# Attention: the three bf16 parts of the negated row maxima laid out as part, head, tile, and turned into rows by one TensorE transpose of 48 columns instead of four of 12

## What is computed

```python
attn = einsum('bhqd,bhkd->bhqk', q, k) * scale          # layer 1
attn = where(causal, attn, -inf)
a = clip(attn, -100.0, 100.0)
m = max(a, axis=-1, keepdims=True)
e = exp(a - m)
p = e / (sum(e, axis=-1, keepdims=True) + 1e-06)
p = p + 1e-08
attn = p / sum(p, axis=-1, keepdims=True)

scores = einsum('bqhd,bkhd->bhqk', q, k) * scale        # layers 2 and 4
probs = softmax(scores, axis=-1)
```

## Time and profile before

| | us |
|---|---|
| median of 3 runs | 2610.97 |
| lowest and highest | 2608.83 and 2614.83 |
| the profiled execution | 2617.94 |
| its span, first to last instruction | 2616.2 |

### The profile page before, as it was taken

How to read it: one execution, slowest core, us unless ns; L and a number is a source line. 1 busy time by engine, 2 the same in 40 slices (tenths; PEclk the granted TensorE clock), 3 DMA queues, 4 the chain that set the end, 5 groups by cost and what they waited for, 6 DMA issues and landing times. The chain is left out here.

```text
span 2616.2 us, 46472 instructions
## 1 busy us (share of the span) xinstructions
PE 2440.0 (93%) x15044; PEld 1418.3 (54%) x15044; DVE 1836.5 (70%) x3685; ACT 1439.2 (55%) x2991; POOL 1350.9 (52%) x1358
## 2 busy tenths in 40 slices
PE   6999999999999999989899699987999999989998
PEld 3555555554444444349799366653344444358897
DVE  4989998999778888844343558867778888844333
ACT  3666666666777777653233223214777777653332
POOL 5356665563234545445555569843334445435555
PEclk8999999999999999999999789988999999999999
DMA  5333333333434444234555200015434444245554
GB/s 159 100 100 108 105 102 105 111 99 101 118 110 132 130 128 124 84 114 166 199 181 174 70 1 17 17 54 138 119 110 128 129 129 125 72 134 168 182 196 139
DMA packets 249938, 305.91 MB, mean 117 GB/s; under 512 B 28034, under 2 KB 224865, under 8 KB 249700
## 3 DMA queue, kind: packets, MB, share of 16 engines
q1 hardware_dynamic: 238164, 275.37, 35.2%
q0 software_dynamic: 10176, 26.27, 2.8%
q10 hardware_dynamic: 1360, 1.31, 0.2%
HBM read 210.32 MB, written 92.84 MB: 116 GB/s over the span
## 5 line engine op out<-in xcount | busy, mean ns | idle before, releaser
L769 DVE TENSOR_REDUCE neg_max_af<-sc_af 128x1 f32<-128x512 f32 (+3 forms) x864 | 551.8, 665 | 111.7 <-PE sc_af L474 85.1
L690 ACT ACTIVATE prob_af<-sct_af 128x512 f32<-128x512 f32 (+1 forms) x864 | 484.9, 582 | 250.5 <-PE sct_af L495 138.1
L769 DVE TENSOR_REDUCE neg_max_f<-sc_f 128x1 f32<-128x512 f32 x512 | 334.2, 685 | 92.4 <-PE sc_f L474 89.6
L690 ACT ACTIVATE prob_f<-sct_f 128x512 f32<-128x512 f32 x512 | 291.3, 598 | 137.0 <-PE sct_f L495 134.8
L474 PE MATMUL sc_af<-stack_k_af,stack_q_af 96*128 96x512 bf16 (+3 forms) x1024 | 331.9, 344 | 18.4 <-DVE neg_max_af L769 13.6
L495 PE MATMUL sct_af<-stack_q_af,stack_k_af 99*128 99x512 bf16 (+3 forms) x1024 | 331.5, 346 | 6.3 <-ACT prob_af L690 4.9
L1599 PE MATMUL y_ps_e<-w_r,hT_e 128*128 x1120 | 258.6, 384 | 8.8 <-issue 5.0
L798 DVE SCALAR_TENSOR_TENSOR prob_af<-prob_af,w_r 128x512 f32<-128x512 f32 (+2 forms) x224 | 231.9, 1043 | 25.9 <-ACT prob_af L690 25.7
L526 PE MATMUL out_af<-prob_af,v_aug_af 128*32 128x512 f32 (+3 forms) x2048 | 232.3, 525 | 6.8 <-DVE prob_af L798 5.9
L1599 PEld LDWEIGHTS y_ps_e<-w_r,hT_e 128*128 128x128 f32 x1120 | 209.6, 192 | 39.8 <-issue 13.3
L495 PEld LDWEIGHTS sct_af<-stack_q_af,stack_k_af 99*128 99x128 bf16 x1024 | 100.1, 98 | 229.8 <-ACT prob_af L690 147.7
(11 more groups left out here) (382 smaller groups left out, 4732.3 us busy)
## 6 DMA issues: line engine op xcount, KB each, us to landing
w_r<-in_f_W_dram SPq DMA_DIRECT2D x66, 1024.0 KB, 6.4
stack_k_af<-k_parts_d SPq DMA_DIRECT2D x64, 384.0 KB, 4.2
k_parts_d<-parts_af SPq DMA_DIRECT2D x187, 128.0 KB
q_parts_d<-parts_af SPq DMA_DIRECT2D x96, 128.0 KB
stack_q_af<-q_parts_d SPq DMA_DIRECT2D x64, 192.0 KB, 3.0
stack_k_f<-k_parts_d SPq DMA_DIRECT2D x32, 384.0 KB, 4.3
w_next<-in_f_W_dram SPq DMA_DIRECT2D x12, 1024.0 KB
k_parts_d<-parts_f SPq DMA_DIRECT2D x91, 128.0 KB
```

The source lines that it names most:

```text
L690: nc.scalar.activation(dst, src.rearrange("p (h q) -> p h q", h=len(heads)), ACT.Exp).then_inc(S.exp_done, 1)
L769: nc.vector.tensor_reduce(M.neg_max[:, qt, heads[0]:heads[-1] + 1], src, AX.X, ALU.max, negate=True).then_inc(S.max_done, 1)
```

## The change

In split_max the three parts are written to a tile laid out part, head, tile. TensorE makes one transpose of all 48 columns into [48, 128]. ScalarE reads [48, 128]. max_sb becomes 48 partitions of 128 tokens, and the DMA of line 292 stands as it was in the code but now takes 48 rows of 256 bytes instead of 12 of 1024; the order part, head, tile, token is that of the three rows it fills. Semaphores, counts and places in the order are the same.

```diff
--- before.py
+++ after.py
@@ -433,9 +433,8 @@
                         last.then_inc(S.y_ps, 1)
                 elif what == "max":
                     pe.wait_ge(S.max_split, 4 * (NG * n + j + 1))
-                    Gb = M.gen_bf[bank_of[use]]
-                    for t in range(KT):
-                        last = nc.tensor.transpose(Gb[0:12, t * P:t * P + P], M.max_parts[:, t, :, :].rearrange("p a h -> p (a h)"), C.ident_bf[:, :])
+                    last = nc.tensor.transpose(M.gen_bf[bank_of[use]][0:12 * KT, 0:P], M.max_parts[:, :, :, :].rearrange("p a h t -> p (a h t)"),
+                                               C.ident_bf[:, :])
                     if causal(n) and j == 1:
                         pe.wait_ge(S.v_total, n + 1)
                         last = nc.tensor.matmul(G[:, D:2 * D], C.ones[:, :], M.v_tot[:, :], start=True, stop=True)
@@ -652,7 +651,7 @@
                     pn, pg = group(n, j - 2)
                     if exists(pn):
                         act.wait_ge(S.max_rows[pg], 16 * (pn + 1))
-                    nc.scalar.activation(M.max_sb[:, j % 2, :], M.gen_bf[bank_of[use]][0:12, 0:T], ACT.Copy).then_inc(S.max_sb, 1)
+                    nc.scalar.activation(M.max_sb[:, j % 2, :], M.gen_bf[bank_of[use]][0:12 * KT, 0:P], ACT.Copy).then_inc(S.max_sb, 1)
 
             def read_qk(use, full):
 
@@ -777,13 +776,14 @@
                 if NG * n + g > 0:
                     dve.wait_ge(S.max_ps, NG * n + g)
                 st = 4 * (NG * n + g)
-                nc.vector.tensor_copy(M.max_parts[:, :, 0, :], M.neg_max[:, :, :]).then_inc(S.max_split, 1)
+                parts = [M.max_parts[:, p, :, :].rearrange("p h t -> p t h") for p in range(3)]
+                nc.vector.tensor_copy(parts[0], M.neg_max[:, :, :]).then_inc(S.max_split, 1)
                 dve.wait_ge(S.max_split, st + 1)
-                nc.vector.tensor_tensor(M.max_rest[:, :, :], M.neg_max[:, :, :], M.max_parts[:, :, 0, :], ALU.subtract).then_inc(S.max_split, 1)
+                nc.vector.tensor_tensor(M.max_rest[:, :, :], M.neg_max[:, :, :], parts[0], ALU.subtract).then_inc(S.max_split, 1)
                 dve.wait_ge(S.max_split, st + 2)
-                nc.vector.tensor_copy(M.max_parts[:, :, 1, :], M.max_rest[:, :, :]).then_inc(S.max_split, 1)
+                nc.vector.tensor_copy(parts[1], M.max_rest[:, :, :]).then_inc(S.max_split, 1)
                 dve.wait_ge(S.max_split, st + 3)
-                nc.vector.tensor_tensor(M.max_parts[:, :, 2, :], M.max_rest[:, :, :], M.max_parts[:, :, 1, :], ALU.subtract).then_inc(S.max_split, 1)
+                nc.vector.tensor_tensor(parts[2], M.max_rest[:, :, :], parts[1], ALU.subtract).then_inc(S.max_split, 1)
 
             def clip(n, g, kt, half):
 
@@ -1246,8 +1246,8 @@
 
     M.neg_max = sb("neg_max", [P, KT, 4])
     M.max_rest = sb("max_rest", [P, KT, 4])
-    M.max_parts = sb("max_parts", [P, KT, 3, 4], BF16)
-    M.max_sb = sb("max_sb", [12, 2, T], BF16)
+    M.max_parts = sb("max_parts", [P, 3, 4, KT], BF16)
+    M.max_sb = sb("max_sb", [12 * KT, 2, P], BF16)
     M.prob = sb("prob", [P, 2, 4, T])
     M.o_sb = sb("o_sb", [P, T])
     M.floor_w = sb("floor_w", [P, KT, 4])
```

## The result

Timed beside each other, the kernel before took 2612.14 us (median of four runs, 2608.83 to 2614.83) and the changed one 2588.83 (four runs, 2581.74 to 2596.38): ratio 0.9919, 95% interval 0.9893 to 0.9944, or 23.3 us less. In a second session, with more runs, it was 2608.39 against 2593.35: ratio 0.994, interval 0.9921 to 0.996, 15.0 us less. The changed kernel is faster; by how much depends on the session more than it should for a change this small, and a part of what follows is about that. The profiled execution took 2595.54 us with a span of 2593.8, against 2616.2 before.

What follows compares the result with a forecast made beforehand. TensorE was taken to bound the kernel, sharing the bound with VectorE in the causal layer. Savings of 10.9 us in the second and last layers and 2.7 in the causal one, 13.6 together, took 2611.0 to 2597.4 us; range 2587 to 2606.

Steps and rivals of the forecast that it cites:

- The bound: TensorE saturated in 64 of the 96 splits; bound shared with VectorE in the 32 causal ones.
- A set, 0.17 us: TensorE's transposes in each of 96 sets: three removed at 0.057 us each, both edges of 0.09 staying.
- the load: Stationary operand of 48 columns instead of 12 on TensorE: 4 ns more, 0.3 us over the sets that count.
- s = 9 and s = 13: Causal groups whose set is at these slots: VectorE waits for TensorE, so 16 sets x 0.17 = 2.7 us pass.
- s = 5: Causal group from this slot: a 0.39 us wait for a clip grows by 0.17 us, so nothing is gained.
- s = 1: Causal group from this slot, VectorE at 97%: TensorE's wait grows by 0.17 us, so nothing is gained.
- ScalarE: Its read of [48, 128] takes about 275 ns, sparing 28 us of ScalarE, at no effect on the end.
- VectorE: Four instructions with changed strides: 0 taken; a bound of 4 x 17 ns in 16 causal groups, 1.1 us.
- The DMA: Line 292 with 48 rows of 256 bytes: landing in about 2.2 us plus 0.1, slack 0.78 us, no wait.
- The term of 0.1: Line 292's transfer, same data in four times the pieces: 0.1 us more until landing.
- The slow rival: At floor_row in 31 causal groups, line 292's landing becomes the wait: 2619 or 2647 us; chance 0.07.
- The clock: Causal half-clock windows, 1.7 us each: three more give 2602 us, four fewer 2591; chance 0.17.

## Why the prediction was right

Forecast 2597.4 us with 2587 to 2606 and faster by over 0.2%: measured 2588.83, in the range and faster, 8.6 us below the point. It is near the lower end, 2587, and two of the four runs (2581.74 and 2582.12) lie below it. Step by step:

**The bound.** Right. The later groups pass what TensorE is spared, nearly all of them by the same 0.15 us.

**A set, 0.17 us.** Right in the three steps, 3 x 0.056; wrong in the load. I took 4 ns for 36 more columns from the recorded durations of 12 and 128 columns. With the three transposes put back, the wider load shows once in a set, behind its first transpose, as 15 to 16 ns; the last step to the next 512-column matmul is 0.152 us with either width. So a set saves 0.321 - 0.169 = 0.15 us, three steps less these 16 ns. The recorded load rose by 11 ns; it is no measure of what is not covered. The Trainium skill, page "TensorE: Matmul & The Clock Gate", section on LDWEIGHTS, gave by the prediction's estimate 30 ns for those columns; the traces lie between it and mine, and its 2.4 us of loss over 80 sets were 1.3. The cost is 14 ns below that rule and 12 above my reading of the rows.

**The causal layer.** s = 9 and s = 13 passed, as forecast. s = 5 brought nothing, as forecast, but the way was different. In the forecast the wait for the clip grows by the whole saving. It grew by 0.04 us:

```profile
289.33 1.06 PE L525 MATMUL out_af<-prob_af,v_aug_af 128*32 128x512 f32 x8 [0.43 <-DVE prob_af L798]
```

against 0.39 in the earlier trace rows; the rest went to a step that was not in the forecast, a weight load that now comes early and waits for ScalarE's exp to free its bank, so that the scores after the first start 0.36 us behind it (287.80 to 288.16) where it was 0.23:

```profile
288.15 0.10 PEld L494 LDWEIGHTS sct_af<-stack_q_af,stack_k_af 99*128 99x128 bf16 x1 [0.24 <-ACT prob_af L689]
```

s = 1 is the step that failed: "There the wait grows by 0.17 us and the 16 sets bring nothing." Half of the 16, those from s = 1, passed 0.16 each, 1.3 us. The two waits there are what they were in the earlier trace rows, 0.51 and 0.49:

```profile
279.73 0.39 PE L473 MATMUL sc_af<-stack_k_af,stack_q_af 96*128 96x512 bf16 x1 [0.51 <-DVE neg_max_af L768]
280.67 0.64 PE L525 MATMUL out_af<-prob_af,v_aug_af 128*32 128x256 f32 x8 [0.49 <-DVE prob_af L798]
```

I had read VectorE's 97% as a chain of fixed length. It isn't one: the length of its clips goes with GpSimd, and GpSimd's start goes with TensorE. One clip of 512 columns takes 1.24 us before and with the three transposes put back, and 1.08 after. In order: before, after, three more transposes:

```profile
281.32 1.24 DVE L798 SCALAR_TENSOR_TENSOR prob_af<-prob_af,w_r 128x512 f32<-128x512 f32 x1
```

```profile
276.74 1.08 DVE L798 SCALAR_TENSOR_TENSOR prob_af<-prob_af,w_r 128x512 f32<-128x512 f32 x1
```

```profile
278.37 1.24 DVE L801 SCALAR_TENSOR_TENSOR prob_af<-prob_af,w_r 128x512 f32<-128x512 f32 x1
```

GpSimd's split of q and k runs beside it (before, after, and with seven more transposes, followed there by the same clip):

```profile
280.86 1.16 POOL L1050 TENSOR_TENSOR parts_af<-qkf_af,parts_af 128x512 bf16<-128x512 f32 x1 [0.16 <-ACT parts_af L668]
```

```profile
276.12 1.15 POOL L1050 TENSOR_TENSOR parts_af<-qkf_af,parts_af 128x512 bf16<-128x512 f32 x1
```

```profile
279.12 1.15 POOL L1053 TENSOR_TENSOR parts_af<-qkf_af,parts_af 128x512 bf16<-128x512 f32 x1 [0.40 <-ACT parts_af L670]
...
279.35 1.47 DVE L801 SCALAR_TENSOR_TENSOR prob_af<-prob_af,w_r 128x512 f32<-128x512 f32 x1
```

Counted from the start of its set, the clip starts at 7.43 us in all three. One digit finer than the lines show, it ends 0.545 to 0.550 us behind the end of GpSimd's instruction, in these three and in every group from s = 1 of the seven steady batches in all 13 profiles. GpSimd's instruction waits for ScalarE's copy out of PSUM, and that copy follows TensorE: it starts 6.21 us behind the set's start in the kernel before, 6.06 in the changed one and 6.45 with seven more transposes. So by these traces what TensorE is spared reaches VectorE through ScalarE and GpSimd. The clip right behind the set shows the other side: it starts 0.15 us earlier and ends where it ended, 3.95 us after the set and 0.81 to 0.82 behind another instruction of GpSimd, which did not move; it takes 1.65 us for 1.50, and 1.26 with seven more transposes. The ends go together in every profile; no run changed GpSimd's work alone, so by what means it holds a clip is left open. After the change GpSimd waits at most 0.01 us there in most batches, where it waited 0.16, so a further saving would not pass in this group by this way; that is an estimate from these rows.

**The two errors cancel.** 0.15 instead of 0.17 over 64 + 16 sets is about 1.5 us less, s = 1 is 1.3 more: with the 0.02 of s = 5, 13.2 us direct, where 13.6 were forecast. That the direct gain comes so near is luck: the two errors have nothing to do with each other.

**ScalarE.** 257 ns for 275, and worth nothing at the end, shown by making the read long again.

**VectorE.** 44 ns a set (11, 11 and 22 ns on three of the four instructions), where I had 0 with 4 x 17 as the bound; no group shows it, since three transposes back give the distances of before plus the 0.016 us of the load.

**The DMA.** No new wait. The one at the start, 0.81 us in the earlier trace rows, is 0.31:

```profile
68.83 0.76 SPq L292 DMA_DIRECT2D stack_q_af<-max_sb_af  x1
...
71.11 0.38 PE L508 MATMUL sct_af<-stack_q_af,stack_k_af 3*128 3x512 bf16 x1 [0.31 <-DMA stack_q_af<-max_sb_af]
```

In the steady batches nothing waits for it. The load of the rows and its reader in a causal batch, beside the earlier trace rows:

```profile
271.36 0.72 SPq L292 DMA_DIRECT2D stack_q_af<-max_sb_af  x1
...
274.36 0.38 PE L508 MATMUL sct_af<-stack_q_af,stack_k_af 3*128 3x512 bf16 x1
```

3.00 us, in the forecast's 2.9 to 3.2, and issuing takes 0.72 as before. The reader at the start, which waits for the landing, starts 71.11 - 68.83 = 2.28 us after the issue, where it was 2.20: 0.08 us more. By the packets of the trace the last one ends 1.69 us after that issue, where it was 1.60, and 1.68 for 1.61 in the steady batches. The term of 0.1 stands. The slow rival is out.

**The clock.** This rival was given 0.17 apart from the forecast, and it came on top of it: two to four causal windows fewer, 2.4 to 4.8 us. Its reason was half right (the windows stand in the group from s = 1 and go with the length of the groups), its direction was left open, and the price of 1.7 us each is 1.2 once the group behind has caught up.

With it, 13.2 + 2.4 to 4.8 makes 15.6 to 18.0 us. The attention stretches of the five profiles agree: sets 1 to 64 and 65 to 96 sum to 1585.5 us in before and 1583.5 in its second profile, and to 1569.1, 1562.6 and 1572.0 in the changed kernel, means 1584.5 and 1567.9, 16.6 apart, though the three of the changed kernel spread over 9.4 us. Of the 22.4 us between the first two profiles, 16.4 lie there, -1.2 at both ends, and 7.2 between sets 64 and 65, where the changed kernel also took 644.9 and before also 657.8: scatter of the clock. Its share was not in the forecast, and the first session's 23 us should not all be credited to the change; the second session's 15.0 is nearer.

## What to carry to other kernels

A small matmul's price is read from distances of starts, with the edges before and behind it; removing three of four saves the steps and leaves the edges, and putting the small one beside another with a narrow load saves an edge more (0.10 us a set here). Where two engines share the bound, do not take "97% busy" for a fixed chain: compare the length of each of its instructions before and after, look whose end their ends follow, and put dummy work back to see which groups pass it on. Compare the stretches that a change touches, cut at the same instruction in each run: here one untouched stretch scattered by 20 us, more than the change was worth.

## What the runs showed of the hardware that was not expected

- A matmul of 128 columns with a narrow load in a row of such costs 0.056 us, with 12 or 48 columns as stationary operand; the load of 48 shows only at the first of the row, whose step is 0.073 us where it is 0.058 with 12, while the recorded loads differ by 11 ns.
- In front of such a matmul a 512-column one takes 0.31 us instead of 0.22, with 48 columns as with 12; with two narrow-load neighbours (48 and 32 columns) the extra is paid once.
- The stretches of 3.4 us at 1.2 GHz in the causal layer come in the same group of a batch each time, their number goes with the length of the batch (five at 70.2 to 70.35 us, none to three at 69.84, two at 71.02), and they cost 1.2 us each, less than half their length.
- The same VectorE clip of 512 columns took 1.08, 1.24 or 1.47 us from the same start, and each time ended 0.55 us behind the end of the GpSimd instruction beside it; one further back ended 0.81 to 0.82 us behind its own, whether it started 2.30 or 2.69 us after the set.
